# Attention head loop on one core: order of scores, masks and value product on TensorE

## What is computed

```python
Q, K = (_rope(Q), _rope(K))
scores = jnp.einsum('bhqd,bhkd->bhqk', Q, K) / jnp.sqrt(jnp.asarray(D_KV, x.dtype))
causal = jnp.tril(jnp.ones((s, s), bool))
scores = jnp.where(causal, scores, jnp.asarray(-jnp.inf, scores.dtype))
attn = jax.nn.softmax(scores, axis=-1)
out = jnp.einsum('bhqk,bhkd->bhqd', attn, V)
```

## Time and profile before

| | us |
|---|---|
| median of 3 runs | 2242.03 |
| lowest and highest | 2226.98, 2248.45 |
| the profiled execution | 2230.01 |
| its span, first to last instruction | 2228.2 |
| TensorE busy in it | 1951.1 (88%) |
| VectorE busy | 1646.1 (74%) |
| ScalarE busy | 1393.5 (63%) |
| mean granted TensorE clock | 0.939 of full |

### The profile page before, as it was taken

The page is one execution under the profiler, slowest core; times in us unless marked ns, Lnnn a source line. Parts: engine busy times, 40 slices in busy tenths (PEclk is TensorE's granted clock), DMA queues, the critical chain, the costliest instruction groups (busy, mean ns, idle before and its releaser), DMA issues.

```text
span 2228.2 us, 40224 instructions
## 1 busy us (share of the span) xinstructions
PE 1951.1 (88%) x12147; PEld 1541.0 (69%) x12147; DVE 1646.1 (74%) x3846; ACT 1393.5 (63%) x3599; POOL 973.9 (44%) x1025
## 2 busy tenths in 40 slices
PE   5797979886995669999899998999989998799995
PEld 5555555556673558888777887788877886577772
DVE  4667676666345679999899998999989996754444
ACT  1454555452341558888878888788887886245560
POOL 0121212121672105554355665566654666177551
PEclk8899999895898789999999999999999999899998
DMA  4157575759234124444334553445534452745557
GB/s 131 44 192 305 214 295 217 279 221 413 94 103 140 43 98 151 150 150 150 132 129 159 173 166 132 135 150 176 173 122 133 164 167 76 215 139 176 158 146 280
DMA packets 143440, 372.59 MB, mean 167 GB/s; under 512 B 22112, under 2 KB 67552, under 8 KB 140928
## 3 DMA queue, kind: packets, MB, share of 16 engines
q1 hardware_dynamic: 128016, 328.36, 43.0%
q0 software_dynamic: 15216, 41.67, 5.5%
HBM read 232.68 MB, written 137.27 MB: 166 GB/s over the span
## 4 chain that ended last, share of the span: by engine, by line
PE 72%; DVE 15%; ACT 5%; issue 3%; DMA 2%; POOL 1%; SPq 1%; POOLq 0%; DVEq 0%; ACTq 0%
PE bank L2163 14%; PE bank L2219 8%; PE bank L2191 5%; PE bank L2600 5%; PE bank L2204 3%; PE bank L2212 3%; PE bank L795 3%; PE bank L1089 3%; PE bank L780 3%; PE bank L2637 2%; PE bank L2177 2%; PE bank L1118 2%; DVE cv L2330 2%; PE bank L804 2%; PE bank L2186 2%
## 5 line engine op out<-in xcount | busy, mean ns | idle before, releaser
L2163 PE MATMUL bank<-h_hi,wi 128*128 128x512 f32 x1024 | 402.0, 434 | 1.3 <-ACTq L151 1.3
L2254 ACT ACTIVATE l_mat<-l_mat,cum_tok 128x128 f32<-128x128 f32 x1024 | 315.1, 424 | 0.0
L2330 DVE SCALAR_TENSOR_TENSOR cv<-bank,cw,cv 128x511 f32<-128x511 f32 (+2 forms) x384 | 287.4, 748 | 32.1 <-ACT cv L2260 13.5
L2383 POOL TENSOR_TENSOR xdec<-xdt,dec_tok 128x384 f32<-128x384 f32 x128 | 107.8, 842 | 384.8 <-DVE xdt L2320 351.6
L2398 POOL TENSOR_TENSOR yg<-yd,sgt 128x512 f32<-128x512 f32 x128 | 227.1, 1775 | 45.8 <-DVE yd L2337 45.8
L2219 PE MATMUL bank<-wo,yg 128*128 128x256 f32 x1024 | 242.4, 380 | 1.5 <-POOL yg L2398 1.5
L2163 PEld LDWEIGHTS bank<-h_hi,wi 128*128 128x128 f32 x1024 | 194.1, 190 | 61.5 <-issue 23.2
L2163 PE MATMUL bank<-h_lo,wi 128*128 128x512 f32 x512 | 202.5, 396 | 0.0
L2219 PEld LDWEIGHTS bank<-wo,yg 128*128 128x128 f32 x1024 | 184.8, 190 | 21.9 <-POOL yg L2398 1.9
L2391 POOL TENSOR_TENSOR gates<-gates,sq 128x512 f32<-128x512 f32 x128 | 164.2, 1283 | 71.9 <-ACT sq L2271 71.8
L693 ACT ACTIVATE work<-bank,nmax 128x512 f32<-128x512 f32 (+3 forms) x256 | 121.0, 530 | 86.8 <-DVE nmax L596 85.6
(11 more groups left out here) (416 smaller groups left out, 4587.6 us busy)
## 6 DMA issues: line engine op xcount, KB each, us to landing
sorted_rows<-blank SPq DMA_DIRECT2D x16, 4644.0 KB, 31.9
wi<-in_weights_split SPq DMA_DIRECT2D x128, 512.0 KB, 3.9
l_mat<-running_sums SPq DMA_DIRECT2D x128, 512.0 KB, 4.9
experts_got<-chosen_rows SPq DMA_DIRECT2D x32, 512.0 KB, 9.4
wo<-out_weights_normed SPq DMA_DIRECT2D x128, 128.0 KB
experts_xt<-sorted_rows SPq DMA_DIRECT2D x127, 129.0 KB, 2.3
w_raw<-in_wi SPq DMA_DIRECT2D x32, 256.0 KB, 2.7
in_weights_split<-w_hi SPq DMA_DIRECT2D x32, 256.0 KB, 2.9
```

The lines of the kernel that those rows point to most:

```text
L2163: mm = e.matmul(dst[:, :], l, r[:, k, tok], start=(n == 0), stop=(n == 3 * KD - 1))
L2254: last = e.activation(part, part, ACT.Relu, bias=cum_tok[:, c, hh, bass.ds(w.g, 1)], scale=-1.0)
L2330: e.scalar_tensor_tensor(out=cv[:, w.two, n:SEQ], in0=PSX[w.two][:, 0:SEQ - n], scalar=cw[:, bass.ds(w.f, 1), TAPS - 1 - n], in1=cv[:, w.t ...
```

## The change

Three things are altered in `attn_pe`, and one table is added. The scores of units 1 and 2 of a head stand together and their masks behind them; a unit's masks are one matmul, which writes to all the unit's diagonal blocks (in unit 1 blocks 0 and 3 of its bank, read from mask_a with a repeat). The value product `heads_of` of a pass stands in front of the next head's first scores instead of behind. Three kinds of waits are left out: on the exponentials ahead of unit 0's scores and ahead of the transposes (except the last head's), and on the copies ahead of the value product (except for the last four heads).

```diff
--- before.py
+++ after.py
@@ -483,6 +483,7 @@
 
     TUNITS = [[(0, 0)], [(1, 0), (3, 384)], [(2, 0)]]
     PART_OF = {0: 0, 1: 1, 3: 1, 2: 2}
+    DIAGONAL = [slice(3, 4), slice(0, 4, 3), slice(1, 2)]
     KOFF = {0: 0, 1: 512, 3: 896, 2: 1024}
     TOFF = [(0, 512), (512, 512), (1024, 256)]
 
@@ -770,8 +771,6 @@
                 mm.then_inc(s_tr, 1)
             t.together()
             def scores(h, u):
-                if u == 0 and h >= 2:
-                    e.wait_ge(s_exp, b * (3 * HEADS) + 3 * (h - 2) + 1)
                 if u and h >= 1:
                     e.wait_ge(s_exp, b * (3 * HEADS) + 3 * (h - 1) + u + 1)
                 rows = slice(SLOT * (h % 2), SLOT * (h % 2) + SLOT)
@@ -779,14 +778,15 @@
                     w = P * (q + 1)
                     e.matmul(score_bank(h, u)[:, col:col + w], qt[rows, h // 2, q * P:(q + 1) * P],
                              kt[rows, h // 2, 0:w], start=(n == 0), stop=False, skip_group_check=True)
-                for q, col in UNITS[u]:
-                    w = P * (q + 1)
-                    last = e.matmul(score_bank(h, u)[:, col + w - P:col + w], ident_b[:, :], mask_a[:, :],
-                                    start=False, stop=True, skip_group_check=True)
-                last.then_inc(s_s, 1)
+
+            def masked(h, u):
+                blocks = score_bank(h, u)[:, :].rearrange("p (c t) -> p c t", t=P)[:, DIAGONAL[u], :]
+                e.matmul(blocks, ident_b[:, :], mask_a[:, :].unsqueeze(1).broadcast_to([P, len(UNITS[u]), P]),
+                         start=False, stop=True, skip_group_check=True).then_inc(s_s, 1)
 
             def turned(g):
-                e.wait_ge(s_exp, b * (3 * HEADS) + 3 * g + 3)
+                if g == HEADS - 1:
+                    e.wait_ge(s_exp, b * (3 * HEADS) + 3 * g + 3)
                 for u, unit in enumerate(TUNITS):
                     if g >= 1:
                         e.wait_ge(s_pt[u], b * HEADS + g)
@@ -797,7 +797,8 @@
                     last.then_inc(s_turn, 1)
 
             def heads_of(g, k):
-                e.wait_ge(s_pt[PART_OF[k]], b * HEADS + 4 * g + 4)
+                if g == HEADS // 4 - 1:
+                    e.wait_ge(s_pt[PART_OF[k]], b * HEADS + 4 * g + 4)
                 if k == 0 and (g or b):
                     e.wait_ge(s_otev, b * 4 + g)
                 for j in range(4):
@@ -807,16 +808,20 @@
                 last.then_inc(s_pv, 1)
 
             scores(0, 0)
+            masked(0, 0)
             for h in range(HEADS + 1):
                 if h < HEADS:
                     scores(h, 1)
                     scores(h, 2)
+                    masked(h, 1)
+                    masked(h, 2)
                 if h >= 1:
                     turned(h - 1)
+                if h >= 6:
+                    heads_of((h - 6) // 4, (h - 6) % 4)
                 if h + 1 < HEADS:
                     scores(h + 1, 0)
-                if h >= 6:
-                    heads_of((h - 6) // 4, (h - 6) % 4)
+                    masked(h + 1, 0)
             heads_of(2, 3)
             for k in range(TT):
                 heads_of(3, k)
```

## The result

| | us |
|---|---|
| before, median of 12 runs | 2239.07 (2226.96 to 2249.1) |
| changed, median of 12 runs | 2257.42 (2252.18 to 2262.28) |
| ratio | 1.0087, 95% interval 1.0071 to 1.0104 |
| changed, in a later series (e14) | 1.0092, interval 1.006 to 1.0124 |

The change costs 18.3 us between the medians, 0.8% (0.9% by the ratio); 18.5 had been forecast. The two profiled executions are further apart: 2230.0 before, near the low end of its runs, and 2262.3 changed, the highest of its twelve. So the 32 us between the profiles are not all the change's. In them 29.0 us have gathered by the last head's first score of group 4 (478.84 before, 507.81 changed), and 3.3 come behind it, where no instruction is changed. One execution of e13 (2581.34 us, granted clock 0.723 where the others had 0.926 to 0.929) is slow and left out of its median and ratio.

A forecast was written before the change was run, and what follows sets the result against it. The prediction took the head loop to be bound by unit 0's round trip through VectorE and ScalarE back to TensorE. Moved product +20.3, masks -1.8 and waits 0 gave +18.5 on 2242.0, so 2260.5 us, range 2243 to 2277.

The forecast's parts named there:

- The regime below pass 6: Head loop, passes 2 to 5, without value product: period stays 3.51 us, set by unit 0's loop through VectorE and ScalarE.
- The product on the loop: Value product before the next first score adds its length to periods from pass 6: net +5.07 us a group, +20.3 for four.
- Rival 1: TensorE's clock falls in the new gaps of the head loop: +18 us more, 2278; chance 0.09.
- a sign that it was wrong: Clock of 0.5 in head-loop periods from pass 6 would show the forecast wrong.
- Masks and scores together: Joined scores and masks of units 1 and 2: 0 at full clock, 0.3 us in six half-clock periods, -1.8 us.
- Removed waits: Left-out waits, 41 a group, repeat ones TensorE has passed: worth 0, at 0.01 us each on the path -1.6 us.
- The sum: Whole kernel: +20.3 - 1.8 = +18.5 us, other stages only later.
- Rival 2: TensorE's own work bounds the head loop, so merged masks count in every pass: 0.25 us each, -16 us, 2226; chance 0.06.
- Rival 3: The order moves in the head loop, but half of the product stays hidden: +9 us, 2251; chance 0.13.

The follow-up runs named there:

- e14: The changed kernel again, unaltered, on the same chip as e13: 2260.88 us in 6 runs, ratio 1.0092 to the old kernel.
- e13: The changed kernel with the old scores and masks of units 1 and 2, product moved and waits left out: 2267.97 us in 5 runs, ratio 1.0125.
- e2: The old kernel with only the value product moved in front of the next first score, masks and waits as before: 2267.05 us in 6 runs, ratio 1.0131.
- e1: The changed kernel with the value product put back behind the next first score, joined masks and removed waits kept: 2236.1 us, ratio 0.9985.
- e4: The changed kernel with each value product between the four transposes to bank 3 and the wait for bank 4, one pass later: 2237.42 us, ratio 0.9988.
- e8: The old kernel with only GpSimd's first weight chunk of each group moved in front of the engines' meeting ahead of the head loop: 2237.28 us, ratio 0.9995.
- e12: The old kernel with only the repeated waits left out: 2242.15 us, ratio 1.0009.
- e6: The changed kernel with the four transposes to bank 3 done twice from pass 7 on, output the same: 2255.2 us in 6 runs, ratio 1.0066.
- e10: The changed kernel with ScalarE's copy of four finished heads behind its copy of bank 4, not in front: 2250.6 us in 9 runs, ratio 1.0046.
- e7: e5 with GpSimd's first weight chunk of each group in front of the engines' meeting ahead of the head loop: 2219.52 us in 8 runs, ratio 0.9916.
- e5: The changed kernel with the next head's first score and mask in front of the transposes, the product behind them: 2232.81 us, ratio 0.9962.
- e11: e7 with ScalarE's copy of four finished heads behind its copy of bank 4, as in e10: 2218.91 us in 6 runs, ratio 0.9915.

## Why the prediction was right

*The regime below pass 6.* Period 3.51, as before; the score to the transposes by the same steps. Right.

*The product on the loop.* +5.41 a group was worked out, nine periods of 38.96. The groups that keep full clock have 38.96 (changed kernel) and 38.98 (e2). From the last score to the product of pass 15 it is 3.51 (156.73 to 160.24), as said. Waits for the copy: 52 in place of 26, "some 50". All right, and e1 and e4 show the cause: the same products cost almost nothing behind the score or in the gap.

*What it really costs* is more than the step's +20.3. The way from e1 to the changed kernel, the same move with the new masks, is 1.0087 less 0.9985, 1.02% or 22.8 us; with the old masks (e2) it is 29. The step left out the fall of the clock behind the longest gap. In the two profiles, nine periods less their falls are 5.41 longer in each group, as worked out, and the falls add 5.1 us in all.

*Rival 1* had 0.09 as a whole of +18. It came true in small: one fall in three of the four groups of the changed kernel's profile and in all four of e14's, at 1.2 to 2.1 us each, 5.1 and 6.4 us in all. The prediction had named half clock there as a sign that it was wrong, and for one or two periods of these groups it was. I had looked at the average gap (0.44, busy 87%) and not at the longest one: eight of the 26 waits of the earlier trace rows are of 0.57 us, in the periods with the copy of heads, and the prediction read all 26 as 0.44. With the product on the loop that copy puts 0.50 on 0.44, and the new masks 0.3: the gap of 1.23.

The longest gap alone doesn't decide it. Passes 7 to 15 of the old kernel, e1, e4, e8 and e12 show no fall, and among them e1 has gaps of 0.87 us and e4 of 1.20 in the same periods, eight times each. What sets them apart is the work before: no gap over 0.2 us in the three periods ahead, where the changed kernel has 0.74 in each. Both cures fit this (e6 shortened all these gaps, e10 the long one), but no run tries the gaps ahead by themselves. Here the Trainium skill (TensorE: Matmul & The Clock Gate, section A second HAM failure mode: psum-queue depth-cycling) warns that short idle times between groups of matmuls, where they come often, make the clock swing. The trace agrees in that all 14 falls of the changed kernel, e14, e2 and e13 stand behind a gap of 0.92 to 1.23 us in a row of shorter ones, and shows no fall with 0.74 in each period (e10) or one of 1.20 by itself (e4).

*Masks and scores together.* Taken as -1.8, six half-clock periods at 0.3. From the third period of a loop on, a half-clock period went from 4.96 to 4.56, so 0.4 each; timeline of TensorE in the changed kernel, second to fourth period:

```profile
96.66 1.11 PE L779 MATMUL bank<-kt,qt 64*128 64x128 f32 x3 [0.67 <-ACT work L694]
...
100.27 0.79 PE L779 MATMUL bank<-kt,qt 64*128 64x512 f32 x1
...
101.21 1.11 PE L779 MATMUL bank<-kt,qt 64*128 64x128 f32 x3
102.26 0.50 PE L784 MATMUL bank<-mask_a,ident_b 128*128 128x256 bf16 x2
102.55 2.34 PE L795 MATMUL bank<-ident,work 128*128 128x128 f32 x10
104.83 0.79 PE L779 MATMUL bank<-kt,qt 64*128 64x512 f32 x1
...
105.71 0.67 PE L779 MATMUL bank<-kt,qt 64*128 64x128 f32 x3
106.31 0.34 PE L784 MATMUL bank<-mask_a,ident_b 128*128 128x256 bf16 x2
106.49 0.61 PE L795 MATMUL bank<-ident,work 128*128 128x128 f32 x4
```

Units 1 and 2 take 1.34 us (101.21 to 102.55) at half clock, where 1.43 was worked out and 1.75 stood in the earlier trace rows, and 0.78 (105.71 to 106.49) at full clock, "about 0.8". But four of the six half-clock periods that were counted are the second of their loop. This one was 5.08 in groups 2 to 4 (5.57 in group 1) and is 5.29 in all groups now, with a new wait of 0.67 us for ScalarE's exponentials (96.66): there the new order loses 0.2 in three groups. The first six periods of a loop are 89.3 us before and 89.6 changed, summed over the four groups, so that the two profiles show no saving.

The runs do say that the term was under-sized: 7.1 us between e13 and e14, 9.6 between e2 and the changed kernel. e1's -3.4 us (interval -8 to +1) doesn't bear on it, since its profile saves 4 x 0.87 us in the product passes, where TensorE was the bound. Part of the difference may be more half-clock periods than six (e12's profile has eleven), but where it lies stays open. No run separates the joined mask from the grouping by kinds of matmul.

*Removed waits.* Put at 0; e12 is 2 us above the old kernel with an interval from -3 to +7, and none of its periods at full clock is shorter or longer. Right as far as it can be told.

*The sum.* +18.5 against 18.3 is closer than its terms. The move was put 2.5 to 9 us too low, and what the masks save, by the pairs, too low by about as much. So the forecast's mechanism was right, and its last digits were luck.

*Rival 2* fell: e1 is 0.15% under the old kernel, not 0.7%. Its price was also too small by its own numbers: half of 1.07 less 0.48 is 0.30 a pass, not 0.25, so -19 us and not -16; 1.07 less the measured 0.78 is 0.29. *Rival 3* fell: nothing of the product is hidden, as the chain shows.

## What to carry to other kernels

On an engine that works in order, ask of each instruction on which side of the loop's slowest round trip it stands: here work of 0.35 to 0.99 us was almost free behind the instruction that the other engines wait for (1.0 us for 5.4 of products in the old kernel, 0.1 in e1), and cost its full length in front of it. The way to gain is the reverse: with the next first score before the transposes a head loop at full clock is 9 us shorter than the old one, and 8 shorter than e1's, which has the same masks. Before such a gain is counted, look at what else ends at the next meeting of the engines. An engine that finishes a few us ahead and shows no wait (here GpSimd, at 58 to 62 of 65 us) is the next floor, and one small edit that shows no gain by itself (e8) then brings the rest (e7).

## What was not expected of the hardware

Gaps of 0.92 to 1.23 us among dense work were followed by half clock, though not each time: the changed kernel, e14, e2 and e13 have 32 such gaps in 16 loops, and one fall in 14 of the loops. A fall costs 1.1 to 2.1 us. Neither the gap nor the busy time around it decides by itself. The stretch of the changed kernel around its gap has 2.77 busy of 4.00 us and the clock fell behind it; that of e4 has 2.80 with a gap of 1.20, and it never fell. The 4 us ahead of them are 3.26 (128 to 132) and 3.83 us busy (129 to 133).

Dense work doesn't always bring the clock back. Stretches of e5 and e11 at the start of a head loop (length, busy us by engine, clock):

```profile
100.00:130.00 30.00, 29.60 (x112) 19.55 (x113) 17.20 (x37) 15.57 (x33) 10.47 (x12) 0.50 0.42 141
```

```profile
300.00:324.00 24.00, 23.28 (x88) 16.04 (x88) 14.67 (x33) 12.49 (x27) 8.27 (x9) 0.50 0.40 142
```

TensorE is busy 97 to 99% of these 24 and 30 us and stays at 1.2 GHz. In the other groups of these two kernels full clock comes back during the third period. What decides it was not tried. Such a loop is about 10 us longer (57.3 and 55.4 in place of 46.1 and 45.7), and it may make much of the spread between runs: the fastest run of e5, 2220.63 us, has a mean granted clock of 0.931, the slowest, 2244.15, has 0.918.
